# Attention layer on one core: where the matmul operands lie in SBUF, modulo 64 bytes

## The chip, the cores and the metric

The kernel runs on 1 core of one Trainium2 chip (trn2). The metric is device time in microseconds (us). Engines are named as in the profile: PE is TensorE (matmuls), PEld its weight loads, DVE VectorE, ACT ScalarE, POOL GpSimd, SP SyncE. A matmul on PE has a *stationary* operand (128 columns, put into the array by a weight load) and a *moving* operand (up to 512 columns, streamed through it). "fp32r" is a 4-byte type in which PE takes a value in one pass.

## The reference

For each of 32 images x of 1024 tokens by 256 channels, all in float32:

```python
def _L0_conv_ref(inputs, Wq, bq, Wk, bk, Wv, bv, Wo, bo):
    ...
    q = x @ Wq + bq
    k = x @ Wk + bk
    v = x @ Wv + bv
    scores = jnp.einsum('bnc,bmc->bnm', q, k) * scale
    attn = jax.nn.softmax(scores, axis=-1)
    attended = jnp.einsum('bnm,bmc->bnc', attn, v)
    out = attended @ Wo + bo
...
x = x + _L0_conv_ref(_gn(x), ...)
```

`_gn` is a group norm over 32 groups of 8 channels, without learned scale.

## The kernel before

The weights are folded once: a = Wq Wk^T and vo = Wv Wo, so that per image there are four families of matmuls. Each float32 operand is split in two fp32r parts, hi and lo, and each product is the sum of three: hi*hi, hi*lo, lo*hi. h is the normalised image (channels on the partitions), N = 1024 tokens, T = 8 tiles of 128 tokens, K = 2 tiles of 128 channels, CH = 2 chunks c of Q = 512 query tokens, TQ = 4 tiles of 128 queries in a chunk.

| family (function, line) | stationary | moving | matmuls per image | columns moved |
|---|---|---|---|---|
| `project_g` (L626 to L638) | a_hi, a_lo | h_hi, h_lo | 24 | 512 |
| `scores` (L654 to L664) | h_hi, h_lo | g_hi, g_lo | 96 (48 per chunk) | 512 |
| `project_v` (L640 to L652) | h_hi, h_lo | vo_hi, vo_lo | 48 | 256 |
| `attend` (L666 to L683) | p_hi, p_lo | v_hi, v_lo | 192 (24 per query tile) | 258 or 256 |

In `attend` there are three matmuls for each key tile m of 0 to 7: L679 (p_hi with v_hi, 258 columns), L680 (p_hi with v_lo, 256) and L681 (p_lo with v_hi, 258). Column 256 of v_hi is 1.0, so that it sums the softmax's denominator; column 257 is zero. The first three families issue their matmuls in the helper `product` (L593), so their rows have that line; the operands' names tell them apart. A row names the output, then the moving and the stationary operand: `ps_s<-g_hi,h_lo` is a score matmul with h_lo stationary.

The order on PE for image b, written out in `body` (L712 to L728): scores of chunk 0; attend of image b-1, chunk 1; project_v; scores of chunk 1 (with the two small group-statistics products `mean_of_groups` and `variance_of_groups` for image b+1 between); attend of chunk 0; project_g of image b+1. The images run in a loop but for the first and the last.

The other engines work beside it. ACT moves scores out of PSUM into s_buf (L306), computes the exponentials p_hi (L314) and once more in float32 (L320), and the hi parts of h, g and v (L289, L294, L299). DVE computes maxima (L435 and on), subtracts them (L465), takes the lo parts (p_lo L473, h_lo L408, g_lo L415, v_lo L421) and finishes the output (L480, L485). PE waits by semaphore for g_lo ahead of scores (L657, L660), for h_lo ahead of project_g (L629), for v_lo and p_lo ahead of attend (L669, L678).

The buffers are allocated in the order in which `sb(...)` names them (L86 to L125), one after the other from byte 16,512 of each partition, each rounded up to 32 bytes. `minus_half` has 8 bytes and takes 32, and this moves what follows it half of 64 bytes on, until `g_bias`, another one of 8 bytes, moves it back. The places that result, in bytes beyond a multiple of 64:

| buffer | used as | before | changed |
|---|---|---|---|
| a_hi, a_lo | stationary | 32 | 0 |
| h_hi, h_lo | stationary in scores and project_v, moving in project_g | 0 | 0 |
| p_hi, p_lo | stationary | 0 | 0 |
| vo_hi, vo_lo | moving | 32 | 32 |
| g_hi, g_lo | moving | 0 | 32 |
| v_hi, row m | moving | 8m (rows of 1032 bytes) | 32 (rows of 1088 bytes) |
| v_lo, row m | moving | 0 (rows of 1024 bytes) | 32 |
| s_buf, x_t, row_max, top2, out_bias | DVE and ACT only | 0 | 0 |
| o_buf | DVE and DMA | 32 | 32 |

The stationary slices are 512 bytes (128 columns of 4 bytes) at multiples of 512 bytes in their buffer, and the moving slices of g, h, vo and v_lo start at multiples of 1024, so that the table holds for each matmul.

The lines of the allocation that matter:

```python
86         ident = sb("ident", [P, P])
...
89         minus_half = sb("minus_half", [P, K])
90         a_hi = sb("a_hi", [P, K, C], F32R)
...
94         g_bias = sb("g_bias", [P, K])
95         out_bias = sb("out_bias", [P, C])
...
103        v_hi = sb("v_hi", [P, T, VC], F32R)
104        v_lo = sb("v_lo", [P, T, C], F32R)
```

Of the kernel before, what the change touches and what calls it, by code (L numbers as in the profile page):

```python
# [31 lines left out]
F32 = mybir.dt.float32  # L32
F32R = mybir.dt.float32r
# [4 lines left out]
P = 128  # L38
# [4 lines left out]
def attention_kernel(nc, x, x_turned, wq, bq, wk, bk, wv, bv, wo, bo, out):  # L43
    B, H, W, C = x.shape
    N = H * W
    T = N // P
    K = C // P
    CH = 2
    Q = N // CH
# [6 lines left out]
    QB = Q // SQ  # L56
    SB = 4
    VC = C + 2
    SCALE = float(C) ** -0.5


# [3 lines left out]
    with ExitStack() as ctx:  # L65
        def sb(name, shape, dt=F32):
            return ctx.enter_context(nc.sbuf_tensor(name, shape, dt))

        def sem(name):
            return ctx.enter_context(nc.semaphore(name))  # L70
# [15 lines left out]
        ident = sb("ident", [P, P])  # L86
        group_mean = sb("group_mean", [P, P])
        ones = sb("ones", [P, P])
        minus_half = sb("minus_half", [P, K])
        a_hi = sb("a_hi", [P, K, C], F32R)  # L90
        a_lo = sb("a_lo", [P, K, C], F32R)
        vo_hi = sb("vo_hi", [P, K, C], F32R)
        vo_lo = sb("vo_lo", [P, K, C], F32R)
        g_bias = sb("g_bias", [P, K])
        out_bias = sb("out_bias", [P, C])


        x_t = sb("x_t", [P, K, N])
        h_hi = sb("h_hi", [P, K, N], F32R)
        h_lo = sb("h_lo", [P, K, N], F32R)  # L100
        g_hi = sb("g_hi", [P, K, N], F32R)
        g_lo = sb("g_lo", [P, K, N], F32R)
        v_hi = sb("v_hi", [P, T, VC], F32R)
        v_lo = sb("v_lo", [P, T, C], F32R)
        bn_parts = sb("bn_parts", [P, K, 2, 6])
        chan = sb("chan", [P, K, 2])
        g_mean = sb("g_mean", [P, K])
# [5 lines left out]


        s_buf = [sb(f"s_buf{c}", [P, T, Q]) for c in range(CH)]
        p_hi = [sb(f"p_hi{c}", [P, T, Q], F32R) for c in range(CH)]
        p_lo = [sb(f"p_lo{c}", [P, T, Q], F32R) for c in range(CH)]
        top2 = sb("top2", [P, 2, Q])
        top_turned = sb("top_turned", [P, Q])
        part_max = sb("part_max", [P, QB])  # L120
# [17 lines left out]
        const_step = sem("const_step")  # L138
# [44 lines left out]
        def after(eng, semaphore, value):  # L183

            if not isinstance(value, int) or value > 0:
                eng.wait_ge(semaphore, value)

        def nothing(*_):
            pass

        def images(eng, body):

            body(0, True, False)
            with eng.Fori(1, B - 1) as b:
                body(b, False, False)
            body(B - 1, False, True)


        @block.sync
        def _(sp):  # L200
            def load_turned(b):
                after(sp, h_lo_done, b * 2)
                for k in range(K):
                    sp.dma_start(x_t[:, k, :], x_turned[b, k * P:(k + 1) * P, :]).then_inc(xt_landed[k], 16)

            def residual(b, c):

                after(sp, x_copied[c], b * 16)
                sp.dma_start(out_v[b, :, c * TQ:(c + 1) * TQ, :],
                             x_v[b, :, c * TQ:(c + 1) * TQ, :]).then_inc(x_copied[c], 16)  # L210

            def load_weight(n, w, landed):
                sp.dma_start(raw[:, n, :, :], w.rearrange("(k p) n -> p k n", p=P)).then_inc(landed, 16)  # L213

            load_weight(0, wq, wqk_in)
            load_weight(1, wk, wqk_in)
            with nc.allow_non_contiguous_dma(reason="a short vector, once"):
                sp.dma_start(bq_col, bq.rearrange("(k p) -> p k", p=P)).then_inc(wqk_in, 16)
            load_turned(0)
            load_weight(2, wv, wvo_in)  # L220
            load_weight(3, wo, wvo_in)
            with nc.allow_non_contiguous_dma(reason="a short vector, once"):
                sp.dma_start(bv_col, bv.rearrange("(k p) -> p k", p=P)).then_inc(wvo_in, 16)
            sp.dma_start(bo_row, bo.rearrange("(a n) -> a n", a=1)).then_inc(wvo_in, 16)
            residual(0, 0)
            residual(0, 1)

            def body(b, first, last):
                if not last:
                    load_turned(b + 1)  # L230
                    residual(b + 1, 0)
                    residual(b + 1, 1)

            images(sp, body)
            after(sp, x_copied[0], 16 * B)
            after(sp, x_copied[1], 16 * B)
            after(sp, stored[0], 16 * B)
            after(sp, stored[1], 16 * B)


        @block.gpsimd
        def _(pool):
            pool.memset(ident[:], 0.0).then_inc(const_step, 1)
            pool.memset(group_mean[:], 1.0 / GC).then_inc(const_step, 1)
            pool.memset(ones[:], 1.0).then_inc(const_step, 1)
            pool.memset(minus_half[:], -0.5).then_inc(const_step, 1)
            pool.memset(v_hi[:, :, C:C + 1].bitcast(F32), 1.0).then_inc(const_step, 1)
            pool.memset(v_hi[:, :, C + 1:VC].bitcast(F32), 0.0).then_inc(const_step, 1)
            pool.wait_ge(const_step, 6)
            pool.affine_select(out=ident[:], in_=ident[:], compare_op=ALU.not_equal, fill=1.0, base=0,  # L250
                               pattern=[[-1, P]], channel_multiplier=1).then_inc(const_step, 1)
            blocks = group_mean[:].rearrange("p (g c) -> p g c", c=GC)
            pool.affine_select(out=blocks, in_=blocks, compare_op=ALU.is_ge, fill=0.0, base=0,
                               pattern=[[-GC, P // GC], [0, GC]], channel_multiplier=1).then_inc(const_step, 1)
            pool.wait_ge(const_step, 8)
            pool.affine_select(out=blocks, in_=blocks, compare_op=ALU.is_ge, fill=0.0, base=GC - 1,
                               pattern=[[GC, P // GC], [0, GC]], channel_multiplier=-1).then_inc(const_step, 1)

            def store(b, c):

                after(pool, x_copied[c], b * 16 + 16)
                after(pool, o_out, b * 8 + (4 * c + 4))
                pool.dma_start(out_v[b, :, c * TQ:(c + 1) * TQ, :], o_buf[c][:],  # L263
                               accum_op=ALU.add).then_inc(stored[c], 16)

            def inverse_std(b):
                pool.wait_ge(var_done, b + 1)
                pool.tensor_tensor(rstd[:], g_var[:], minus_half[:], ALU.pow).then_inc(rstd_done, 1)

            inverse_std(0)  # L270

            def body(b, first, last):
                if not first:
                    store(b - 1, 1)
                if not last:
                    inverse_std(b + 1)
                store(b, 0)

            images(pool, body)
            store(B - 1, 1)  # L280
# [3 lines left out]
        def _(act):  # L284
# [23 lines left out]
            def exponentials_hi(b, c, i):  # L308

                rows = slice(i * PIECE, (i + 1) * PIECE)  # L310
                if i == 0:
                    after(act, o_ps, b * 8 + (4 * c + 4 - 8))
                act.wait_ge(diff_done, b * 8 + (4 * c + i + 1))
                nc.scalar.activation(p_hi[c][:, rows, :], s_buf[c][:, rows, :], ACT.Exp,  # L314
                                     scale=SCALE).then_inc(p_hi_done, 1)

            def exponentials(b, c, i):

                piece = s_buf[c][:, i * PIECE:(i + 1) * PIECE, :]
                nc.scalar.activation(piece, piece, ACT.Exp, scale=SCALE).then_inc(p_done, 1)  # L320

# [267 lines left out]
        def _(pe):  # L589
# [76 lines left out]
            def attend(b, c, j, last_image=False):  # L666

                if j == 0:
                    pe.wait_ge(v_lo_done, b * 4 + 4)  # L669
                if j >= 2:  # L670

                    after(pe, o_out, b * 8 + (4 * c + j + 1 - 4))
                    if c == 0 and not last_image:
                        pe.wait_ge((spread_done, var_done)[j - 2], b + 2)
                ps, cols = ps_o[j], slice(j * P, (j + 1) * P)
                for m in range(T):
                    if j == 0 and m % PIECE == 0:
                        pe.wait_ge(p_lo_done, b * 8 + (4 * c + m // PIECE + 1))  # L678
                    nc.tensor.matmul(ps[:, 0:VC], p_hi[c][:, m, cols], v_hi[:, m, :], start=m == 0, stop=False)  # L679
                    nc.tensor.matmul(ps[:, 0:C], p_hi[c][:, m, cols], v_lo[:, m, :], start=False, stop=False)  # L680
                    last = nc.tensor.matmul(ps[:, 0:VC], p_lo[c][:, m, cols], v_hi[:, m, :], start=False,  # L681
                                            stop=m == T - 1)
                last.then_inc(o_ps, 1)  # L683

# [46 lines left out]
            for j in range(TQ):  # L731
                attend(B - 1, 1, j)
# [31 lines left out]
```

## Time and profile before

| | |
|---|---|
| median of 3 runs | 1859.79 us (1859.34 to 1862.06) |
| the profiled execution | 1862.75 us, its span 1861.1 us, mean granted clock 0.994 |
| PE busy | 1833.9 us (99% of the span) in 11690 matmuls |
| PEld busy | 1670.2 us (90%) |
| DVE busy | 1642.1 us (88%) |
| ACT busy | 981.8 us (53%) |
| POOL busy | 94.0 us (5%) |
| DMA | 101.92 MB, mean 55 GB/s |

Matmuls are pipelined: a row's duration is longer than the time until the next one starts (0.39 us against 0.23 us for 512 columns). What a matmul takes of the span is therefore read from start to start, in the timeline, and not from its mean duration. The granted clock is given in shares of 2.4 GHz.

### The profile page before, as it was taken

To read this page: it belongs to the slowest core of one execution; us is meant where nothing else is said; L and a number is where in the kernel's file an instruction comes from. 1 tells how busy PE (TensorE), PEld (TensorE's weight loads), DVE (VectorE), ACT (ScalarE), POOL (GpSimd) and SP (SyncE) were. 2 spreads that over 40 slices of the span, in tenths; PEclk is the share of its full clock that TensorE was granted. 3 is DMA by queue.
4 is the path that set the end of the run, shared out by engine and by line. 5 is a ranking of instruction groups with operands and counts; after the bars stand their busy time and mean duration, and the time that the engine had idled before them with its cause. 6 is when DMAs were issued, how large, how long until landed. Compare 5 with 4: busy or idle time off the path is not lost.

```text
span 1861.1 us, 33031 instructions
## 1 busy us (share of the span) xinstructions
PE 1833.9 (99%) x11690; PEld 1670.2 (90%) x11690; DVE 1642.1 (88%) x2793; ACT 981.8 (53%) x1347; POOL 94.0 (5%) x109
## 2 busy tenths in 40 slices
PE   8899999999999999999999999999999999999997
PEld 7799998998998998989999989989889999899896
DVE  5898998988988989989889889889899898898885
ACT  3545545546546455456455465465564554654652
POOL 0000000000000000000000000000000000000000
PEclk9899999999999999999999999999999999999998
DMA  3211212202222112222122222132221122220211
GB/s 113 57 44 36 68 56 68 68 19 60 68 56 68 55 24 68 56 68 68 32 47 68 56 68 62 17 68 60 64 68 36 42 68 56 68 67 12 67 23 24
DMA packets 29296, 101.92 MB, mean 55 GB/s; under 512 B 3681, under 2 KB 4706, under 8 KB 29282
## 3 DMA queue, kind: packets, MB, share of 16 engines
q0 software_dynamic: 9216, 33.56, 11.6%
q1 hardware_dynamic: 20066, 68.17, 11.2%
q8 instruction: 9, 0.15, 0.0%
q14 instruction: 5, 0.04, 0.0%
HBM read 68.16 MB, written 67.11 MB: 73 GB/s over the span
## 4 chain that ended last, share of the span: by engine, by line
PE 98%; DVE 1%; ACT 0%; DMA 0%; issue 0%; SPq 0%; POOLq 0%
PE ps_s L593 48%; PE ps_o L681 13%; PE ps_o L679 13%; PE ps_o L680 13%; PE ps_o L593 10%; DMA s_buf<-in_L_conv_bq_dram 0%; ACT p_hi L314 0%; ACT s_buf L320 0%; DVE s_buf L465 0%; DVE p_lo L473 0%; PE ps_o L605 0%; DVE s_buf L490 0%; DVE query_max L452 0%; PE ps_s L605 0%; SPq L213 0%
## 5 line engine op out<-in xcount | busy, mean ns | idle before, releaser
L679 PE MATMUL ps_o<-v_hi,p_hi 128*128 128x258 f32 x2048 | 580.5, 283 | 3.2 <-DVE p_lo L473 3.2
L681 PE MATMUL ps_o<-v_hi,p_lo 128*128 128x258 f32 x2048 | 582.0, 284 | 0.0
L680 PE MATMUL ps_o<-v_lo,p_hi 128*128 128x256 f32 x2048 | 578.1, 282 | 0.0
L314 ACT ACTIVATE p_hi<-s_buf 128x1024 fp32r<-128x1024 f32 x256 | 272.1, 1063 | 527.2 <-DVE s_buf L465 527.2
L593 PE MATMUL ps_s<-g_hi,h_hi 128*128 128x512 f32 x1024 | 406.3, 397 | 7.5 <-ACT s_buf L306 7.5
L593 PE MATMUL ps_s<-g_hi,h_lo 128*128 128x512 f32 x1024 | 400.8, 391 | 0.0
L593 PE MATMUL ps_s<-g_lo,h_hi 128*128 128x512 f32 x1024 | 399.6, 390 | 0.0
L679 PEld LDWEIGHTS ps_o<-v_hi,p_hi 128*128 128x128 f32 x2048 | 387.5, 189 | 6.1 <-issue 2.2
L680 PEld LDWEIGHTS ps_o<-v_lo,p_hi 128*128 128x128 f32 x2048 | 389.7, 190 | 2.8
L306 ACT ACTIVATE s_buf<-ps_s 128x512 f32<-128x512 f32 x512 | 293.6, 608 | 185.5 <-PE ps_s L593 182.8
L681 PEld LDWEIGHTS ps_o<-v_hi,p_lo 128*128 128x128 f32 x2048 | 388.5, 190 | 0.0
L473 DVE TENSOR_TENSOR p_lo<-s_buf,p_hi 128x1024 fp32r<-128x1024 f32 x256 | 304.3, 1219 | 22.7 <-ACT s_buf L320 22.7
L465 DVE TENSOR_TENSOR s_buf<-s_buf,row_max 128x1024 f32<-128x1024 f32 x256 | 306.5, 1218 | 1.1
L320 ACT ACTIVATE s_buf<-s_buf 128x1024 f32<-128x1024 f32 x256 | 271.1, 1059 | 0.0
L593 PEld LDWEIGHTS ps_s<-g_hi,h_hi 128*128 128x128 f32 x1024 | 192.9, 188 | 45.9 <-ACT s_buf L306 7.8
L435 DVE TENSOR_TENSOR top<-top,s_buf 128x512 f32<-128x512 f32 (+1 forms) x192 | 166.8, 869 | 75.4 <-ACT s_buf L306 64.1
L593 PEld LDWEIGHTS ps_s<-g_hi,h_lo 128*128 128x128 f32 x1024 | 192.7, 188 | 42.0
L593 PEld LDWEIGHTS ps_s<-g_lo,h_hi 128*128 128x128 f32 x1024 | 193.1, 189 | 37.1
L485 DVE SCALAR_TENSOR_TENSOR o_buf<-ps_o,rden,out_bias 128x256 f32<-128x256 f32 x256 | 123.9, 484 | 14.4
L263 POOL DMA_DIRECT2D out_dram<-o_buf x64 | 55.9, 874 | 1366.7 <-DVE o_buf L485 1349.5
L299 ACT ACTIVATE v_hi<-ps_o 128x512 fp32r<-128x512 f32 x64 | 38.4, 600 | 107.3 <-PE ps_o L593 107.3
L435 DVE TENSOR_TENSOR top<-s_buf 128x1024 f32<-128x1024 f32 x64 | 78.4, 1225 | 12.1 <-ACT s_buf L306 12.1
(86 smaller groups left out, 2213.4 us busy)
## 6 DMA issues: line engine op xcount, KB each, us to landing
x_t<-in_x_turned_dram SPq DMA_DIRECT2D x64, 512.0 KB, 4.0
out_dram<-in_x_dram SPq DMA_DIRECT2D x64, 512.0 KB, 7.6
out_dram<-o_buf POOLq DMA_DIRECT2D x64, 512.0 KB, 5.4
s_buf<-in_L_conv_Wq_dram SPq DMA_DIRECT2D x1, 256.0 KB, 3.1
s_buf<-in_L_conv_Wk_dram SPq DMA_DIRECT2D x1, 256.0 KB, 3.1
s_buf<-in_L_conv_Wv_dram SPq DMA_DIRECT2D x1, 256.0 KB
s_buf<-in_L_conv_Wo_dram SPq DMA_DIRECT2D x1, 256.0 KB
s_buf<-in_L_conv_bq_dram SPq DMA_DIRECT2D x1, 1.0 KB, 4.0
```

Of the source, the lines that this page charges most:

```text
L263: pool.dma_start(out_v[b, :, c * TQ:(c + 1) * TQ, :], o_buf[c][:], accum_op=ALU.add).then_inc(stored[c], 16)
L306: nc.scalar.activation(s_buf[c][:, m, :], ps_s[(8 * c + m) % SB][:], ACT.Copy).then_inc(s_out, 1)
L314: nc.scalar.activation(p_hi[c][:, rows, :], s_buf[c][:, rows, :], ACT.Exp, scale=SCALE).then_inc(p_hi_done, 1)
L320: nc.scalar.activation(piece, piece, ACT.Exp, scale=SCALE).then_inc(p_done, 1)
L435: nc.vector.tensor_tensor(to, left, right, ALU.max).then_inc(top_step, 1)
L465: nc.vector.tensor_tensor(piece, piece, row_max[:].unsqueeze(1).broadcast_to([P, PIECE, Q]), ALU.subtract).then_inc(diff_done, 1)
L473: nc.vector.tensor_tensor(p_lo[c][:, rows, :], s_buf[c][:, rows, :], p_hi[c][:, rows, :].bitcast(F32), ALU.subtract).then_inc(p_lo_done, 1)
L485: nc.vector.scalar_tensor_tensor(out=o_buf[c][:, j, :], in0=ps_o[j][:, 0:C], scalar=rden[:, t:t + 1], in1=out_bias[:], op0=ALU.mult, op1=A ...
L593: last = nc.tensor.matmul(ps, stationary, moving, start=start and n == 0, stop=stop and n == len(pairs) - 1)
L679: nc.tensor.matmul(ps[:, 0:VC], p_hi[c][:, m, cols], v_hi[:, m, :], start=m == 0, stop=False)
L680: nc.tensor.matmul(ps[:, 0:C], p_hi[c][:, m, cols], v_lo[:, m, :], start=False, stop=False)
L681: last = nc.tensor.matmul(ps[:, 0:VC], p_lo[c][:, m, cols], v_hi[:, m, :], start=False, stop=m == T - 1)
```

## The change

The allocation is reordered. First come the buffers that are stationary in some matmul (and x_t), from a multiple of 64 bytes; then a filler `shift` of 32 bytes; then the buffers that are only moving operands (vo, g, v_hi, v_lo); then a filler `shift_back` of 32 bytes, and the rest. A row of v_hi is 272 columns (1088 bytes, 17 times 64) in place of 258 (1032 bytes); the matmuls still read the first 258, and the start-up memset of the columns behind the ones is 15 columns wide in place of 1. No instruction is added, dropped or moved on any engine, and all shapes on PE, DVE and ACT stay.

```diff
+    VROW = 272
...
-        minus_half = sb("minus_half", [P, K])
+
         a_hi = sb("a_hi", [P, K, C], F32R)
         a_lo = sb("a_lo", [P, K, C], F32R)
-        vo_hi = sb("vo_hi", [P, K, C], F32R)
-        vo_lo = sb("vo_lo", [P, K, C], F32R)
-        g_bias = sb("g_bias", [P, K])
-        out_bias = sb("out_bias", [P, C])
-
-
         x_t = sb("x_t", [P, K, N])
         h_hi = sb("h_hi", [P, K, N], F32R)
         h_lo = sb("h_lo", [P, K, N], F32R)
+        p_hi = [sb(f"p_hi{c}", [P, T, Q], F32R) for c in range(CH)]
+        p_lo = [sb(f"p_lo{c}", [P, T, Q], F32R) for c in range(CH)]
+
+        sb("shift", [P, 8])
+        vo_hi = sb("vo_hi", [P, K, C], F32R)
+        vo_lo = sb("vo_lo", [P, K, C], F32R)
         g_hi = sb("g_hi", [P, K, N], F32R)
         g_lo = sb("g_lo", [P, K, N], F32R)
-        v_hi = sb("v_hi", [P, T, VC], F32R)
+        v_hi = sb("v_hi", [P, T, VROW], F32R)
         v_lo = sb("v_lo", [P, T, C], F32R)
+        sb("shift_back", [P, 8])
+
+        minus_half = sb("minus_half", [P, K])
+        g_bias = sb("g_bias", [P, K])
+        out_bias = sb("out_bias", [P, C])
...
-        p_hi = [sb(f"p_hi{c}", [P, T, Q], F32R) for c in range(CH)]
-        p_lo = [sb(f"p_lo{c}", [P, T, Q], F32R) for c in range(CH)]
...
-            pool.memset(v_hi[:, :, C + 1:VC].bitcast(F32), 0.0).then_inc(const_step, 1)
+            pool.memset(v_hi[:, :, C + 1:VROW].bitcast(F32), 0.0).then_inc(const_step, 1)
...
-                    nc.tensor.matmul(ps[:, 0:VC], p_hi[c][:, m, cols], v_hi[:, m, :], start=m == 0, stop=False)
+                    nc.tensor.matmul(ps[:, 0:VC], p_hi[c][:, m, cols], v_hi[:, m, 0:VC], start=m == 0, stop=False)
...
-                    last = nc.tensor.matmul(ps[:, 0:VC], p_lo[c][:, m, cols], v_hi[:, m, :], start=False,
+                    last = nc.tensor.matmul(ps[:, 0:VC], p_lo[c][:, m, cols], v_hi[:, m, 0:VC], start=False,
```

## Rows read from the trace of the kernel before

**Rows 1.** The page: engines' busy time, and the chain of waits by engine and line

```profile
PE 1833.9 (99%) x11690; PEld 1670.2 (90%) x11690; DVE 1642.1 (88%) x2793; ACT 981.8 (53%) x1347; POOL 94.0 (5%) x109
...
PE 98%; DVE 1%; ACT 0%; DMA 0%; issue 0%; SPq 0%; POOLq 0%
```

**Rows 2.** Timeline of PE: first matmul of six stages; start us, duration us, name, count

```profile
887.21 0.29 PE L679 MATMUL ps_o<-v_hi,p_hi 128*128 128x258 f32 x1
...
898.74 0.28 PE L593 MATMUL ps_o<-vo_hi,h_hi 128*128 128x256 f32 x1
...
904.42 0.40 PE L593 MATMUL ps_s<-g_hi,h_hi 128*128 128x512 f32 x1
...
915.85 0.29 PE L679 MATMUL ps_o<-v_hi,p_hi 128*128 128x258 f32 x1
...
927.37 0.40 PE L593 MATMUL ps_o<-h_hi,a_hi 128*128 128x512 f32 x1
...
932.98 0.39 PE L593 MATMUL ps_s<-g_hi,h_hi 128*128 128x512 f32 x1
...
943.88 0.29 PE L679 MATMUL ps_o<-v_hi,p_hi 128*128 128x258 f32 x1
```

**Rows 3.** Timeline of PE: one query tile of attend, L679 of key tiles 0, 1, 3, 4, 5

```profile
892.96 0.28 PE L679 MATMUL ps_o<-v_hi,p_hi 128*128 128x258 f32 x1
...
893.33 0.28 PE L679 MATMUL ps_o<-v_hi,p_hi 128*128 128x258 f32 x1
...
894.05 0.28 PE L679 MATMUL ps_o<-v_hi,p_hi 128*128 128x258 f32 x1
...
894.42 0.28 PE L679 MATMUL ps_o<-v_hi,p_hi 128*128 128x258 f32 x1
...
894.77 0.29 PE L679 MATMUL ps_o<-v_hi,p_hi 128*128 128x258 f32 x1
```

**Rows 4.** Busy time by stretch: attend, then project_g; us, busy (count) by engine, clock

```profile
915.90:927.30 11.40, 11.40 (x97) 11.40 (x96) 10.44 (x22) 2.61 (x3) 0.31 (x1) 1.00 0.00 0
927.40:932.90 5.50, 5.50 (x26) 4.41 (x25) 5.43 (x10) 5.00 (x7) 0.28 (x1) 1.00 0.86 257
```

**Rows 5.** Timeline of PE at the start-up: float32 products in several passes, 256 columns

```profile
16.76 3.19 PE L593 MATMUL ps_s<-s_buf 128*128 128x256 f32 x7
...
19.75 0.63 PE L593 MATMUL ps_o<-s_buf,o_buf 128*128 128x256 f32 x1
```

**Rows 6.** Timeline of DVE beside project_g: start us, duration us, name, count

```profile
924.42 2.31 DVE L408 TENSOR_TENSOR h_lo<-x_t,h_hi 128x1024 fp32r<-128x1024 f32 x2
...
931.91 0.74 DVE L415 SCALAR_TENSOR_TENSOR g_lo<-ps_o,g_bias,g_hi 128x512 fp32r<-128x512 f32 x1
```

**Rows 7.** The waits of PE: waited for, us in total, times, longest us

```profile
PE ps_s L593 <- ACT s_buf L306: 7.5, 1, 7.5
...
PE ps_o L605 <- DMA s_buf<-in_L_conv_bq_dram: 6.0, 1, 6.0
...
PE ps_o L679 <- DVE p_lo L473: 3.2, 2, 2.0
```

**Rows 8.** Timeline of POOL at the start, and the first work of PE

```profile
1.43 0.11 POOL L248 MEMSET v_hi<- 128x8 f32 x1
...
5.98 1.97 PE L605 MATMUL ps_o<-ident,s_buf 128*128 128x128 f32 x8 [5.98 <-DMA s_buf<-in_L_conv_bq_dram]
```

## The prediction

> **What bounds the kernel now.** The page says it at once: PE is busy for 99% of the span, and the chain of work that ended last is PE for 98% of it [rows 1]. PE's list of waits is short; its three longest entries make 16.7 us in all, two of them single events at the start [rows 7]. So what a change does to the time here, it does through how quickly one matmul follows another on PE.
>
> That pace is read from the start times [rows 2], one image in its six stages, each from its first matmul to the next stage's first. Attend of chunk 1: 887.21 to 898.74, 11.53 us for 96 matmuls, 120.1 ns each. project_v: 5.68 us for 48, 118.3 ns. Scores of chunk 1: 11.43 us for 48 and the two small statistics products between them. Attend of chunk 0: 11.52 us for 96, 120.0 ns. project_g: 5.61 us for 24, 233.8 ns. Scores of chunk 0: 932.98 to 943.88, 10.90 us for 48, 227.1 ns. An image takes 56.67 us.
>
> The granted clock is 1.00 of 2.4 GHz [rows 4]. At a column per cycle 512 columns would take 213.3 ns, 256 columns 106.7, and attend's average of 257.3 (two of 258, one of 256) 107.2. What is left over is an **excess per matmul**. Beside it I set the places of the operands modulo 64 bytes, from the table above:
>
> - scores, 512 columns, stationary at 0, moving at 0: 227.1 - 213.3 = 13.8 ns
> - project_g, 512 columns, stationary at 32, moving at 0: 233.8 - 213.3 = 20.5 ns
> - project_v, 256 columns, stationary at 0, moving at 32: 118.3 - 106.7 = 11.6 ns
> - attend, 257.3 columns, stationary at 0, moving at 0 (v_lo) or 8m (v_hi): 120.05 - 107.2 = 12.85 ns
>
> Within attend, the key tiles differ. In one query tile [rows 3] tile m = 0, all operands at 0, takes 893.33 - 892.96 = 0.37 us for its three matmuls. Tile 3, with v_hi at 24, also takes 0.37, and tile 4, with v_hi at 32, only 0.35. The 24 matmuls of this tile (the next query tile starts at 895.85) have nothing else that differs between m = 0 and m = 4. The rows' last digit is 0.01 us, so 0.35 is 115 to 118 ns per matmul, which with rounding on both ends I take as 117.7, an excess of 10.5 ns; 0.37 is 123, an excess near 15. That is the same as for scores (13.8) with twice the columns at the same places.
>
> So the excess reads like a toll per pair of weight load and matmul, not per column, and it depends on where the two operands lie: about 14 to 15 for (0, 0), about 11 for (0, 32), about 20 for (32, 0). The start-up has a stretch without it: seven float32 products of 256 columns, four passes each, take 19.75 - 16.76 = 2.99 us, 427 ns each, which is 4 times 106.7 [rows 5]. There PE draws its moving values at a quarter of the rate beside the loads. The toll seems to be paid where both operands are read from SBUF at full rate.
>
> **The Trainium skill against this.** Its page "TensorE: Matmul & The Clock Gate", section "Part 2: What happens when you issue a matmul", says that TensorE has two independent read ports into SBUF, and that loading the next weights takes no bandwidth from the running matmul. By that rule no place modulo 64 could matter and the change would do nothing; this trace speaks against it, as project_g and scores, of equal shape, differ by 6.7 ns. The page "SBUF — State Buffer", section "Specifications (TRN2)", has 16-byte lines; by it only v_hi's odd rows (8m no multiple of 16) would cross more lines, tile 4 would not differ from tile 0, and little would be won. Tiles 0 and 4 do differ [rows 3].
>
> **The change, part by part.** No instruction is added or moved, so the sum is four families by their new excess. For (stationary 0, moving 32) I have two prices, 11.6 from project_v and 10.5 from key tile 4, and take 11.1.
>
> 1. *attend*, 192 times 32 = 6144 matmuls, goes to (0, 32) throughout: 107.2 + 11.1 = 118.3 in place of 120.05, which is 1.75 ns each, **-10.8 us**. Bounds: 118.8 (project_v's excess), -7.7 us; 116.7 (0.35 us by three), -20.6 us.
> 2. *scores*, 3072 matmuls, g moves from 0 to 32: 213.3 + 11.1 = 224.4 in place of 227.1, 2.7 ns each, **-8.3 us**. This is the term that no row shows: 512 columns at (0, 32). Bounds: below, twice the gain, -16.6 us, if the wider matmul profits for both halves of its stream; above, 233.8, project_g's price, which is also a pair 32 bytes apart, +20.6 us. I take the value near project_v and tile 4, because (0, 0) costs about the same at 512 and at 256 columns, so the width doesn't seem to matter.
> 3. *project_g*, 24 times 32 = 768 matmuls, goes from (32, 0) to (0, 0), because a moves down and h is the moving operand there: 227.1 in place of 233.8, 6.7 ns each, **-5.1 us**. Bounds: 0 if it is the stream h that is dear there, -6 if the toll were 12.9 as in attend.
> 4. *project_v* is (0, 32) before and after: 0.
> 5. *The memset* at the start is wider (15 columns of 8 rows for 1) in an operation of 0.11 us at 1.43; PE starts at 5.98 with the weights' DMA [rows 8]. Even tenfold it ends before. Cost 0, and were the cover gone, at most the 1 us that it grows.
> 6. *DVE and ACT* keep their shapes; g_lo, g_hi, v_lo and v_hi are written 32 bytes on. No row tells the two places of one buffer apart there. I set it at 0: it hides in the slack that follows, and what goes beyond that slack is paid in full.
>
> **What is late next.** DVE is busy 10.44 of 11.40 us beside attend and 5.43 of 5.50 beside project_g [rows 4], and its chain there starts from the last score tile, not from attend. The second g_lo ends at 931.91 + 0.74 = 932.65, and the first score matmul, which waits for it (L657), starts at 932.98: 0.33 us of slack. h_lo ends at 924.42 + 2.31 = 926.73 and project_g starts at 927.37: 0.64 us [rows 6, 2]. The change takes 96 times 1.75 ns = 0.17 us from attend and 24 times 6.7 = 0.16 us from project_g, 0.33 together: the whole slack of g_lo, and no more. If attend came to 116.7 (0.32 us), scores would wait 0.15 us per image, about 5 us in all of the further gain given back.
>
> **Sum.** -10.8 - 8.3 - 5.1 = -24.2 us on the profiled execution, 1862.75 to 1838.6. The median before was 1859.79, 3.0 lower, so the forecast is **1836 us**.
>
> **The rivals.**
>
> *R1, slower: what counts at 512 columns is that the operands are 32 apart.* The only 512-column rows with places 32 apart are project_g's, and they are the slow ones. If the order of the two doesn't matter, then scores, the largest family by columns, turns from 227.1 to 233.8, +20.6 us; project_g gains its 5.1, and attend at project_v's price 7.7: +7.8, that is 1868 us. It decides from the point where a score matmul passes 227.1 + (10.8 + 5.1)/3072 = 232.3 ns. For it: project_g; and 118.3 of project_v doubled is 236.6. Against: the toll of (0, 0) doesn't grow with the columns. Chance 0.20.
>
> *R2, scores stay.* Their pace of 227.1 is the steadiest in the trace and may be a floor of its own for 512 columns. Then only attend and project_g gain: -15.9, 1844 us. Chance 0.13.
>
> *R3, no change.* The tolls follow from something else than the place modulo 64 (higher address bits, the order of the streams), and all buffers move there too, so that gains and losses cancel, or the change doesn't make the difference it states: 1860 us. Against: tile 4 against tile 0, of the same buffers. Chance 0.12.
>
> *R4, the toll goes away.* (0, 32) keeps the two readers apart once all matmuls have it, and the excess falls to 2 or 3 ns as in the start-up's passes [rows 5]: 11 ns from each score matmul and 10 from each of attend would be 1.06 us per image in scores and 0.96 in each attend; of the attend ahead of project_g only the 0.33 us of g_lo's slack can be had, so (1.06 + 0.96 + 0.33) times 32 = 75 us, 1785 us. Against: project_v, 48 in a row at (0, 32), has 11.6. Chance 0.03.
>
> **How the numbers follow.** The forecast itself has 0.52. A measurement of this kernel can tell from no change what is over about 0.2%, 3.7 us. The forecast, R2 and R4 are faster by more: 0.68. R3 is the same: 0.12. R1 is slower: 0.20. The range goes down to 1817, the forecast with attend at 116.7, scores at twice the gain and project_g's 5.1 (-42.3), and up to R1's 1868, of which half lies above; with R4 and the rest of R1 out, some 0.15 is left out. Since cases of both signs are in it: the forecast's own range is 1817 to 1848.
>
> **What would show each step.** In the timeline of PE of the changed kernel, from start to start: attend about 11.36 us for 96 matmuls in place of 11.53, and all key tiles alike (0.35 or 0.36); scores of chunk 0 about 10.77 in place of 10.90; project_g about 5.45 in place of 5.61; project_v still 5.68. An image then takes about 55.9 us in place of 56.67. Scores above 10.95 us say R1; scores at 10.90 with the rest as forecast say R2; all stages as before say R3. A wait of PE for DVE's g_lo, not in the list now, says that the slack was spent. The forecast is wrong if project_v moves, as its places modulo 64 stay, or if key tiles still differ.

## The result and the profile after

The changed kernel takes 1868.47 us (median of 6 runs, 1865.65 to 1869.53) against 1860.94 us of the kernel before (6 runs, 1859.34 to 1862.46): a ratio of 1.004, with a 95% interval of 1.0028 to 1.0052. It is 7.5 us slower. The profiled execution took 1869.22 us, with a span of 1867.6 us and a mean granted clock of 0.995.

The page has PE where it was, at 99% of a longer span, with 7.5 us more of busy time; DVE and ACT are where they were [rows 1]:

```profile
PE 1841.4 (99%) x11690; PEld 1661.5 (89%) x11690; DVE 1644.2 (88%) x2793; ACT 982.5 (53%) x1347; POOL 94.1 (5%) x109
```

The timeline of PE, one image, the first matmul of each stage as in [rows 2] (columns: start us, duration us, name, count):

```profile
946.85 0.28 PE L683 MATMUL ps_o<-v_hi,p_hi 128*128 128x258 f32 x1
...
958.29 0.28 PE L597 MATMUL ps_o<-vo_hi,h_hi 128*128 128x256 f32 x1
...
963.95 0.39 PE L597 MATMUL ps_s<-g_hi,h_hi 128*128 128x512 f32 x1
...
975.57 0.28 PE L683 MATMUL ps_o<-v_hi,p_hi 128*128 128x258 f32 x1
...
987.03 0.40 PE L597 MATMUL ps_o<-h_hi,a_hi 128*128 128x512 f32 x1
...
992.54 0.46 PE L597 MATMUL ps_s<-g_hi,h_hi 128*128 128x512 f32 x1
...
1003.80 0.28 PE L683 MATMUL ps_o<-v_hi,p_hi 128*128 128x258 f32 x1
```

The differences of these starts, beside those of the kernel before and of two kernels that come below (g_back and v64, read in the same way, one image each):

| stage (us) | before | changed | g_back | v64 |
|---|---|---|---|---|
| attend, chunk 1 | 11.53 | 11.44 | 11.47 | 11.32 |
| project_v | 5.68 | 5.66 | 5.60 | 5.44 |
| scores, chunk 1 | 11.43 | 11.62 | 11.43 | 11.39 |
| attend, chunk 0 | 11.52 | 11.46 | 11.47 | 11.31 |
| project_g | 5.61 | 5.51 | 5.51 | 5.66 |
| scores, chunk 0 | 10.90 | 11.26 | 11.01 | 11.02 |
| image | 56.67 | 56.95 | 56.49 | 56.14 |

In this image the score stages lose 0.19 and 0.36 us; everything else gains, 0.27 us together. Added up from start to start over all images, scores went from 707.9 to 724.5 us (+16.6), attend from 744.0 to 739.2 (-4.8), project_g from 179.5 to 176.3 (-3.2), project_v from 181.8 to 180.4 (-1.4): +7.2 us. The two profiled executions differ by 6.5 us and the medians by 7.5.

The time between g_lo and the scores has shrunk, too. DVE's rows beside project_g [rows 6]: the second g_lo ends at 991.63 + 0.74 = 992.37, the first score matmul starts at 992.54, 0.17 us later where it was 0.33.

```profile
984.14 2.32 DVE L412 TENSOR_TENSOR h_lo<-x_t,h_hi 128x1024 fp32r<-128x1024 f32 x2
...
991.63 0.74 DVE L419 SCALAR_TENSOR_TENSOR g_lo<-ps_o,g_bias,g_hi 128x512 fp32r<-128x512 f32 x1
```

That already costs a little. The first score matmul lasts 0.46 us in place of 0.39, and the second follows it only after 0.30 us:

```profile
992.54 0.46 PE L597 MATMUL ps_s<-g_hi,h_hi 128*128 128x512 f32 x1
992.84 0.39 PE L597 MATMUL ps_s<-g_lo,h_hi 128*128 128x512 f32 x1
```

Over the images this first gap averages 276 ns, against 232 ns in only_g (below), whose scores run at the same pace and whose g_lo is early. So about 1.4 of the 16.6 us that scores lose are a wait, and the rest is their pace. In every kernel here the second score matmul starts 0.46 us or more after the end of g_lo. Before the change it started 0.55 to 0.60 us after it, so that only some 0.10 us of the 0.33 could be had.

### The profile page after: what moved, and what is told of

It is laid out like the page before. It is cut to its first block, busy times and chain, and to the rows that moved or that the text cites. A ratio compares the mean times of both kernels' runs of the same rounds, so it can differ in the third digit from the quotient of the medians.

```text
span 1867.6 us, 33031 instructions
## 1 busy us (share of the span) xinstructions
PE 1841.4 (99%) x11690; PEld 1661.5 (89%) x11690; DVE 1644.2 (88%) x2793; ACT 982.5 (53%) x1347; POOL 94.1 (5%) x109
## 4 chain that ended last, share of the span: by engine, by line
PE 98%; DVE 1%; ACT 0%; DMA 0%; issue 0%; SPq 0%; POOLq 0%
PE ps_s L597 49%; PE ps_o L683 13%; PE ps_o L685 13%; PE ps_o L684 13%; PE ps_o L597 10%; DMA s_buf<-in_L_conv_bq_dram 0%; ACT p_hi L318 0%; ACT s_buf L324 0%; DVE s_buf L469 0%; DVE p_lo L477 0%; PE ps_o L609 0%; DVE s_buf L494 0%; DVE query_max L456 0%; PE ps_s L609 0%; SPq L217 0%
## 5 line engine op out<-in xcount | busy, mean ns | idle before, releaser
L597 PE MATMUL ps_s<-g_hi,h_hi 128*128 128x512 f32 x1024 | 411.3, 402 | 7.4 <-ACT s_buf L310 7.4
L597 PE MATMUL ps_s<-g_hi,h_lo 128*128 128x512 f32 x1024 | 405.2, 396 | 0.0
L597 PE MATMUL ps_s<-g_lo,h_hi 128*128 128x512 f32 x1024 | 405.1, 396 | 0.0
```

The lines of the kernel that those rows point to most:

```text
L597: last = nc.tensor.matmul(ps, stationary, moving, start=start and n == 0, stop=stop and n == len(pairs) - 1)
```

## The experiments

"Distance" below is the moving operand's start minus the stationary operand's, in bytes. Three theories stood at first. D: the distance modulo 64 sets the pace. P: any operand off a multiple of 64 costs. T: the toll of the forecast, one price per pair whatever the width. The ratios are of each kernel's runs to those of the kernel before on the same chip. Each kernel of blocks ran once.

### Blocks of equal matmuls: distance or place

The attention is replaced by 35 blocks of 48 matmuls, each with one width and one pair of places:

```diff
+            for i, (cols, s, d, wide) in enumerate(CONFIGS):
+                for n in range(COUNT):
+                    last = nc.tensor.matmul(banks[i % 8][0:wide, 0:cols], left[:, s:s + wide], right[:, d:d + cols],
+                                            start=n == 0, stop=n == COUNT - 1)
+                last.then_inc(done, 1)
```

> Leaves the whole attention out: it copies x to the output and runs 35 blocks of 48 matmuls on constant data, each block with its own width and places of the two operands modulo 64 bytes. Theory D (distance): the pace of a 512-column matmul depends on the distance of the two operands modulo 64. Then (0,0) and (32,32) take 227 ns, (0,32) and (32,0) take 233 to 234. Theory P (place): an operand that starts off a multiple of 64 costs more. Then (32,32) takes 234 or more, up to 240. Theory T (toll per pair, as forecast): (0,32) takes 224 ns. For 256 columns D and P expect 117 to 120 for all, with little between them; T expects 118 for (0,32) and 121 for (0,0).

Timeline of PE within six blocks, 512 columns each (start, time from the first start to the last end, count). The pace is that time less one duration of 0.39 us, by the count less one:

```profile
21.22 5.29 PE L83 MATMUL ps<-right,left 128*128 128x512 f32 x22
...
32.18 5.76 PE L83 MATMUL ps<-right,left 128*128 128x512 f32 x24
...
43.71 5.15 PE L83 MATMUL ps<-right,left 128*128 128x512 f32 x22
...
120.72 6.11 PE L83 MATMUL ps<-right,left 128*128 128x512 f32 x26
...
132.24 5.73 PE L83 MATMUL ps<-right,left 128*128 128x512 f32 x24
...
290.83 5.60 PE L83 MATMUL ps<-right,left 128*128 128x512 f32 x24
```

In order: (stationary 0, moving 32) 4.90/21 = 233 ns; (32, 0) 5.37/23 = 233 ns; (32, 32) 4.76/21 = 227 ns; (0, 64) 5.72/25 = 229 ns; (0, 128) 5.34/23 = 232 ns; (0, 0) 5.21/23 = 227 ns. (32, 32) is as quick as (0, 0), and the two mixed pairs are equal: at 512 columns **it is the distance, and P falls**. T falls with (0, 32), for which it had 224. And a multiple of 64 is not enough: a distance of 128 costs 5 ns, while 256 and 512 bytes gave 226.6, as 0 did.

From the start times of the last 24 matmuls of each block:

| columns | distance 0 | 32 | -32 | 64 | 128 | 256 |
|---|---|---|---|---|---|---|
| 512 | 226.7 ns | 233.3 | 233.2 | 228.7 | 232.2 | 226.6 |
| 384 | 173.3 | 173.3 | | | | |
| 256 | 120.0 | 117.7 | 118.2 | 113.4 | 118.6 | 120.0 |

At 256 columns the order turns round: a distance of 32 is better than 0 by 2.3 ns, and 64 is better by 6.6. Three lines of the same view show it, 256 columns at distance 0, 64 and 128, with durations of 0.28 us: 2.16/18 = 120, 2.26/20 = 113 and 2.26/19 = 119 ns.

```profile
174.33 2.44 PE L83 MATMUL ps<-right,left 128*128 128x256 f32 x19
...
231.39 2.54 PE L83 MATMUL ps<-right,left 128*128 128x256 f32 x21
...
236.83 2.54 PE L83 MATMUL ps<-right,left 128*128 128x256 f32 x20
```

### g alone moved

The kernel before, with a filler on each side of g:

```diff
+        sb("shift", [P, 8])
         g_hi = sb("g_hi", [P, K, N], F32R)
         g_lo = sb("g_lo", [P, K, N], F32R)
+        sb("shift_back", [P, 8])
```

> The kernel before with g alone moved 32 bytes on. Theory D and theory P: scores go from 227 to 233.3 ns, 5.2 to 6 ns on 3072 matmuls, 16 to 18 us slower, and attend, project_v and project_g stay. If the loss of the change sits elsewhere (in attend's new rows or in DVE), this kernel is no more than 5 us slower.

1874.83 us, ratio 1.0076 (1.0061 to 1.0092): 13.6 us slower. Scores of chunk 0 in its timeline of PE: 1006.46 - 995.27 = 11.19 us in place of 10.90.

```profile
995.27 0.39 PE L595 MATMUL ps_s<-g_hi,h_hi 128*128 128x512 f32 x1
...
1006.46 0.28 PE L681 MATMUL ps_o<-v_hi,p_hi 128*128 128x258 f32 x1
```

Scores add up to 723.3 us, 15.5 more; attend got 1.9 us of waits back. So g's 32 bytes by themselves cost more than the whole change loses; its other parts gain.

### g back at a multiple of 64

```diff
+        g_hi = sb("g_hi", [P, K, N], F32R)
+        g_lo = sb("g_lo", [P, K, N], F32R)
         sb("shift", [P, 8])
         vo_hi = sb("vo_hi", [P, K, C], F32R)
         vo_lo = sb("vo_lo", [P, K, C], F32R)
-        g_hi = sb("g_hi", [P, K, N], F32R)
-        g_lo = sb("g_lo", [P, K, N], F32R)
```

> The changed kernel with g back at a multiple of 64 bytes, all else as changed. Theory D and P: scores return to 227 ns, 16 us less than the changed kernel, 1852 to 1853 us, 8 us faster than before: attend's 0.7 ns on 6144 matmuls and project_g's 4.2 ns on 768 stay as gains. If scores were slowed by something else than g's place, it stays near 1868 us.

1854.83 us, ratio 0.9966 (0.9954 to 0.9978): faster than before by 6.4 us and than the changed kernel by 13.6. That is 2 us short of what was expected. The last column but one of the stage table shows where: scores of chunk 0 take 11.01 us, not 10.90. After project_g at its new pace the second g_lo comes just too late: in all images but one the first score matmul starts 0.13 or 0.14 us after it, and the next one follows after 0.33 us in place of 0.23. That is 0.10 us in nearly every image, 3 us. The weight loads (PEld) show what is late: the load of the first score matmul, which before started 0.21 us ahead of its matmul (932.77 for 932.98, [rows 2]), now starts with it, at 984.48 for 984.49.

The kernel before:

```profile
932.77 0.19 PEld L593 LDWEIGHTS ps_s<-g_hi,h_hi 128*128 128x128 f32 x1
```

g_back:

```profile
984.48 0.19 PEld L597 LDWEIGHTS ps_s<-g_hi,h_hi 128*128 128x128 f32 x1 [0.25 <-issue]
...
984.49 0.49 PE L597 MATMUL ps_s<-g_hi,h_hi 128*128 128x512 f32 x1
984.82 0.39 PE L597 MATMUL ps_s<-g_lo,h_hi 128*128 128x512 f32 x1
```

### All operands at distance 0 modulo 64

The changed kernel without the filler `shift` ahead of vo (it stands behind v_lo):

```diff
-        sb("shift", [P, 8])
         vo_hi = sb("vo_hi", [P, K, C], F32R)
...
         v_lo = sb("v_lo", [P, T, C], F32R)
+        sb("shift", [P, 8])
         sb("shift_back", [P, 8])
```

> The changed kernel with every matmul operand at a multiple of 64 bytes, rows of v_hi 1088 bytes apart. Theory D: scores and project_g 227 ns as in g_back; attend and project_v at distance 0. If 256 columns behave as 512 do, attend and project_v gain too, down to 113.5 ns, 4 to 6 ns on 7680 matmuls, 1815 to 1825 us. If key tile 4 of the kernel before (v_hi at 32) showed the better place, attend goes to 121 ns, 10 us above g_back. If 256 columns do not care, it equals g_back, 1852 us.

1858.51 us, ratio 0.9984 (0.9975 to 0.9993), 3.7 us slower than g_back. project_v goes to 120.0 ns, as the block of 256 columns at distance 0 does (g_back: 116.7); attend stays, 119.3 ns without its waits, against 119.5. The hope that 256 columns behave as 512 do fell, and so did the 121 ns for attend.

### v alone moved

The kernel before with v_hi and v_lo at distance 32 modulo 256, as the changed kernel has them:

```diff
+    VROW = 272
...
-        v_hi = sb("v_hi", [P, T, VC], F32R)
+        sb("shift", [P, 40])
+        v_hi = sb("v_hi", [P, T, VROW], F32R)
         v_lo = sb("v_lo", [P, T, C], F32R)
+        sb("shift_back", [P, 40])
```

> The kernel before with v_hi and v_lo alone moved to 32 bytes past a multiple of 64 (and 32 past the stationary operand modulo 256, as in the changed kernel), rows of v_hi 1088 bytes apart; g, a and vo stay. Theory D: scores and project_g stay at 227 and 233.5 ns; attend takes the changed kernel's 119.4 in place of 120.1 ns, 4.3 us faster in all, 1856 to 1857 us. The forecast's toll had attend at 118.3, 10.8 us faster, 1850 us.

1858.99 us, ratio 0.9989 (0.9979 to 0.9998). That is 1.6 us less than the kernel before on the same chip, with an interval from 0.4 to 3.9; attend adds up to 740.8 us, 3.2 less. So v's part of the change is worth 2 to 3 us, not the forecast's 10.8.

### A distance that is a multiple of 64, but not of 256

g_back with g 128 bytes on:

```diff
+        sb("away", [P, 32])
         g_hi = sb("g_hi", [P, K, N], F32R)
         g_lo = sb("g_lo", [P, K, N], F32R)
+        sb("away_back", [P, 32])
```

> The kernel g_back with g moved 128 bytes on: still a multiple of 64, but 128 from h modulo 256. If only the distance modulo 64 counted, nothing changes, 1854.8 us. By the blocks (232.2 ns at a distance of 128 bytes) scores lose 4 to 5 ns on 3072 matmuls, 12 to 15 us: 1867 to 1870 us.

1866.94 us, ratio 1.0033 (1.002 to 1.0046), 12 us slower than g_back, where the distance modulo 64 had it unchanged. Scores of chunk 0 take 1000.88 - 989.68 = 11.20 us. The rule "modulo 64" of the change's own words is too coarse.

```profile
989.68 0.44 PE L599 MATMUL ps_s<-g_hi,h_hi 128*128 128x512 f32 x1
...
1000.88 0.28 PE L685 MATMUL ps_o<-v_hi,p_hi 128*128 128x258 f32 x1
```

### More blocks, and project_v at 192

> Leaves the whole attention out, as the first block kernel, with 36 other blocks; all places are multiples of 64 bytes but for a few near 64. The first block kernel had 256 columns at 120.0 ns for a distance of 0, 256 and 512 bytes, 118.6 for 128 and 113.4 for 64. Theory D256: what counts is the distance modulo 256 bytes. Then 64, 320 and 576 bytes take 113.4 ns, 192, 448 and 704 take another common value, and a stationary operand at 64 with a moving one at 128 (distance 64) takes 113.4 too. Theory place: only a moving operand at 64 bytes itself is fast, and (64, 128) takes 120. For 258 columns, as attend has them, D256 expects about 114.2 at 64 bytes if the two extra columns cost their 0.8 ns only, and 119 to 120 if the pattern is broken by them. 512 columns at distance 64 repeat 228.7.

Timeline of PE in two of these blocks of 256 columns, distances 192 and 320 (2.49/22 = 113 and 2.47/21 = 118 ns):

```profile
13.33 2.77 PE L84 MATMUL ps<-right,left 128*128 128x256 f32 x23
...
18.99 2.75 PE L84 MATMUL ps<-right,left 128*128 128x256 f32 x22
```

At 512 columns the distance modulo 256 sets the pace in all of these blocks. (64, 64) took 226.7 ns as (0, 0) did; (32, 96) took 229.0, the same as (0, 64) in this kernel; (128, 0) took 232.1, as (0, 128) had; (0, 192) and (64, 0), which is 192 modulo 256, took 233.4 both.

At 256 columns it is not so simple. Moving places of 192, 448 and 704 with the stationary operand at 0 all took 113.35 ns, but (64, 0), the same distance modulo 256, took 117.8. 320 and 576 took 117.8, though 64 had taken 113.4 in the first kernel of blocks. (0, 64) itself stood at the start of this kernel: its first 25 matmuls followed one another at about 213 ns, and the rest at 117.8. So the very same places gave 113.4 and 117.8 ns, and how a stretch is entered matters. (64, 128), which was to decide, took 117.8 too, where one theory had 113.4 and the other 120: both fell. No run tells whether (64, 0) differs from (0, 192) by its places or by the block ahead of it. 258 columns at 64 bytes took 118.6, where 114.2 was hoped for: the two extra columns spoil it.

The kernel g_back with vo at 192:

```diff
-        sb("shift", [P, 8])
+        sb("shift", [P, 48])
         vo_hi = sb("vo_hi", [P, K, C], F32R)
         vo_lo = sb("vo_lo", [P, K, C], F32R)
+        sb("more", [P, 24])
```

> The kernel g_back with vo at a distance of 192 bytes from h modulo 256, where blocks of 256 columns took 113.35 ns. project_v then goes from 116.7 to 113.4 ns if it falls into that pattern, 3.3 ns on 1536 matmuls, 5 us faster, 1850 us. If the pattern depends on how the stretch is entered, 117.8 ns, 1.6 us slower than g_back.

1849.22 us, ratio 0.9933 (0.9919 to 0.9946), 5.6 us faster than g_back. project_v takes 954.11 - 948.66 = 5.45 us for 48, and after its first three matmuls each follows at 113 or 114 ns.

```profile
948.66 0.28 PE L598 MATMUL ps_o<-vo_hi,h_hi 128*128 128x256 f32 x1
...
954.11 0.39 PE L598 MATMUL ps_s<-g_hi,h_hi 128*128 128x512 f32 x1
```

### v at 16 bytes: a miss

g_back with v_hi, v_lo and vo starting 4 columns into buffers of their own, and rows of v_hi 1280 bytes apart:

```diff
-    VROW = 272
+    VROW = 320
...
+        def past(name, rows, width, by=4):
+            whole = sb(name, [P, rows * width + 64], F32R)
+            return whole[:, by:by + rows * width].rearrange("p (r w) -> p r w", w=width)
```

> The kernel g_back with v_hi, v_lo and vo 16 bytes past the place of the stationary operand modulo 256 (rows of v_hi 1280 bytes apart), where blocks of 256 and 258 columns took 116.6 and 116.8 ns. Attend then goes from 119.4 to 116.8 ns. Of the 0.25 us per image that the attend ahead of project_g gains, only the 0.13 us that g_lo is early are had, of the other attend all: 12 us faster than g_back, 1843 us. If the three different operands of attend break the pattern, attend stays at 119 to 120 ns and the time within 3 us of g_back.

1875.85 us, ratio 1.008 (1.0066 to 1.0094). Blocks of 256 and 258 columns had taken 116.6 and 116.8 ns at this distance. attend fell into a pattern of 126, 128 and 119 ns and stayed in it, 124 ns on average: here the blocks' pace did not carry over.

The kernel shows one thing more. As attend is slow, g_lo comes 0.51 us ahead of the first score matmul, and chunk 0's scores take 10.88 us, the least of all kernels with g at distance 0. That fits the 11.01 us in g_back as a wait.

### Attend's triple in blocks, then in the kernel

```diff
+                    cols, d = (256, d2) if n % 3 == 1 else (258, d1 + step * (n // 3 % 8))
```

> Leaves the whole attention out, as the block kernels. Each block of 60 matmuls repeats attend's triple: 258, 256 and 258 columns with the stationary operand at 0, the 258-column ones d1 and the 256-column one d2 past it, d1 and d2 of 0, 32, 64, 128 and 192 bytes; five more blocks have 16 bytes, or v_hi's place moving on by 64 bytes from one triple to the next as rows of 1088 bytes do. Attend in the changed kernel takes 119.4 ns. If one row of places is as good for the triple as 192 bytes is for 256 columns alone (113.4 ns), it shows a mean of 115 or less here; if the two extra columns spoil every pattern, as in the blocks of 258 columns, all means lie from 117 to 124 ns. If the order of places matters and not the distance alone, the block of 16 bytes is slow here, at 124, as attend was in v16.

The 30 means lie from 115.6 to 122.2 ns. All four blocks in which v_hi's place moves on by 64 bytes per triple, as rows of 1088 bytes do, have 119.4 to 119.7 over their last 24 gaps, whatever the first distance: that is attend's pace in the changed kernel. With v_hi standing still modulo 256, (32, 32) gives 117.9 and (64, 192) gives 117.8. The block of 16 bytes was the best here, at 115.6, and did not show the 124 of v16. Both good pairs went into the kernel vo192:

```diff
-    VROW = 272
+    VROW = 320
```

and, for the second, more fillers around v_hi and v_lo:

```diff
-        sb("more", [P, 24])
+        sb("more", [P, 32])
         v_hi = sb("v_hi", [P, T, VROW], F32R)
+        sb("more_yet", [P, 32])
         v_lo = sb("v_lo", [P, T, C], F32R)
-        sb("shift_back", [P, 8])
+        sb("shift_back", [P, 32])
```

> The kernel vo192 with rows of v_hi 1280 bytes apart, so that all operands of attend lie 32 bytes past the stationary one modulo 256 for every key tile. In the blocks of triples that took 117.9 ns, against 119.4 to 119.6 for rows that move on by 64 bytes each (and 119.46 in vo192's attend). If the blocks carry over: 1.5 ns on 6144 matmuls, 9 us faster than vo192's 1849 us, 1840 us, with at most 1 us of it given back in a wait for g_lo. If attend keeps a pattern of its own, as in v16, it may be anywhere from 117 to 124 ns, 1835 to 1877 us.

> As row1280, with v_hi 64 and v_lo 192 bytes past the stationary operand modulo 256; in the blocks of triples 117.8 ns, the same as row1280's 117.9. If the blocks carry over, both kernels end within 2 us of each other near 1840 us. If they part by more, blocks of a single stationary slice do not tell what attend does.

row1280: 1850.75 us, ratio 0.9941 (0.9927 to 0.9954). v64: 1842.99 us, ratio 0.9901 (0.9886 to 0.9917), **18.9 us faster than the kernel before**. attend does what the blocks said in both, 117.9 and 117.8 ns. In row1280's timeline its key tiles are all alike at last, 0.35 or 0.36 us each; in the changed kernel they still differ, 0.35 to 0.37:

```profile
945.31 0.28 PE L684 MATMUL ps_o<-v_hi,p_hi 128*128 128x258 f32 x1
...
945.66 0.28 PE L684 MATMUL ps_o<-v_hi,p_hi 128*128 128x258 f32 x1
...
946.02 0.28 PE L684 MATMUL ps_o<-v_hi,p_hi 128*128 128x258 f32 x1
...
946.37 0.28 PE L684 MATMUL ps_o<-v_hi,p_hi 128*128 128x258 f32 x1
```

The changed kernel, the same line:

```profile
949.69 0.28 PE L683 MATMUL ps_o<-v_hi,p_hi 128*128 128x258 f32 x1
...
950.05 0.29 PE L683 MATMUL ps_o<-v_hi,p_hi 128*128 128x258 f32 x1
...
950.42 0.28 PE L683 MATMUL ps_o<-v_hi,p_hi 128*128 128x258 f32 x1
```

row1280 missed its 1840 us: it is 1.5 us slower than vo192. Its attend gained 10.1 us (739.6 to 729.5), but project_v lost 6.3 (174.6 to 180.9) and project_g with the wait behind it 4.8 (176.2 to 181.0).

Why do row1280 and v64 part by 7.8 us? project_v has the same places in both, but comes in from another pattern of attend: in row1280 it runs at 117.8 ns, in v64 at 113.6, 180.9 against 174.5 us. These are the two paces that the blocks showed too. v is also written to other places in the two kernels; no run takes that apart from the way in.

In both the gain of the attend ahead of project_g is given back in a wait for g_lo. In v64's timeline of PE, project_g's last matmul starts at 978.45 and the first of scores at 978.87: 0.42 us for 0.227. Its g_lo ends at 978.00 + 0.74 = 978.74. The second score matmul then follows only after 0.33 us, as in g_back.

```profile
978.45 0.39 PE L599 MATMUL ps_s<-h_hi,a_lo 128*128 128x512 f32 x1
978.87 0.49 PE L599 MATMUL ps_s<-g_hi,h_hi 128*128 128x512 f32 x1
979.20 0.40 PE L599 MATMUL ps_s<-g_lo,h_hi 128*128 128x512 f32 x1
```

```profile
978.00 0.74 DVE L421 SCALAR_TENSOR_TENSOR g_lo<-ps_o,g_bias,g_hi 128x512 fp32r<-128x512 f32 x1
```

That is 0.19 us ahead of the scores and 0.10 us behind the first of them, 0.29 us in nearly every image, 9 us. From here on, DVE's order beside project_g sets part of the time.

## Why the prediction was wrong

**The step that failed is term 2, scores**: forecast -8.3 us, measured +16.6. It took the toll of (0, 32) from 256-column rows and carried it to 512 columns, on the ground that "(0, 0) costs about the same at 512 and at 256 columns, so the width doesn't seem to matter". That ground holds in the blocks, and says nothing of other distances: (0, 0) has 13.3 ns at 256, 384 and 512 columns, but a distance of 32 has 11.1, 13.3 and 20.0. The only 512-column rows with unequal places were project_g's, 20.5 ns [rows 2], and the forecast read them as a matter of which operand was off. The blocks show both orders at 233 ns.

**Rival R1 was what happened**, with its mechanism, and its time of 1868 us within 0.5 us. Its deciding point was 232.3 ns per score matmul; without the jumps at the statistics products they took 233.2. It had been given 0.20, and the range ended at its number, so that the result lies just outside. That its total is so near is partly luck: scores lost 16.6 us where R1 had 20.6, and attend and project_g gained 8.0 together where R1 had 12.8.

*Term 1, attend*: -10.8 forecast, -4.8 measured, 119.4 ns for 118.3. The price came from key tile 4 against tile 0 [rows 3]. But with v_hi at 32 modulo 64 throughout, the tiles still differ: their three matmuls take 354 to 365 ns on average over the images, where it was 353 to 366. The forecast looked at places modulo 64 alone. Modulo 256, tile 0 of the kernel before was no (0, 0): v_hi lay 128 + 8m and v_lo 192 bytes past p. And 1088-byte rows keep moving v_hi on by 64 modulo 256. That a tile's time also carries what the tiles before it left behind is likely from the blocks, but not shown for a single tile. "All key tiles alike" was wrong for the changed kernel and right for row1280.

*Term 3, project_g*: -5.1 forecast, -3.2 measured. It does reach 227 ns, but only after its first 11 matmuls (224 to 240 ns on the way), and there are only 24 in a row.

*Term 4, project_v*: 0 forecast, -1.4 measured, 118.3 to 117.4 ns with its places modulo 64 unchanged. Modulo 256 they did change: vo lay 32 bytes before h's place and now lies 32 bytes past it. The blocks have 118.2 ns for the one and 117.7 for the other, and only_v, which keeps the old places but has the new rows of v, stays at 118.5. The way in has a part as well: g_back, with the changed kernel's places, runs at 116.7.

*Terms 5 and 6*, the memset and the writes of DVE and ACT, were rightly at nothing: DVE's busy time is 1644.2 us for 1642.1.

*What is late next* named the right wait and had its size wrong. Of the 0.33 us between g_lo and the scores only some 0.10 could be had, since the second score matmul never starts sooner than 0.46 us after g_lo. The changed kernel pays 1.4 us for it in the time of its scores, g_back 3, and v64 9, where the forecast had nothing up to 0.33 us. PE's list of waits doesn't show it; the start times do.

*The Trainium skill.* The page "TensorE: Matmul & The Clock Gate", section "Part 2: What happens when you issue a matmul", has two independent SBUF read ports for the two operands. By that alone their distance should not matter. For fp32r it does: between one distance and another, blocks of equal 512-column matmuls differ by 6.6 ns each. The 16-byte lines of "SBUF — State Buffer", section "Specifications (TRN2)", don't explain it either, since all the places in the table above are multiples of 16. Off them, blocks of 256 columns took 126.7 ns at 8 bytes, but 120.0 to 120.1 at 24, 40 and 56, as at 0.

**What stays open.** No run shows what in the chip repeats with 256 bytes, or why the pace depends on history. That the weight load and the moving stream disturb each other is the reading of the start-up's undisturbed passes [rows 5] and of the dependence on distance at 512 columns; no run took the weight loads away.

## What to carry to other kernels

Where back-to-back fp32r matmuls with a weight load each bound the kernel, the distance of the two operands in SBUF is a tuning knob worth about 1%, and it has to be set for each width by itself: here a multiple of 256 bytes for 512 columns and 192 for 256, where 64 was as good in one block and not in others. A price read at one width or one pair of places is no price for another; make blocks of the very shape first, and then run them in the kernel, because a stretch also takes on the pattern of the one before it. And when PE is sped up, look how early each operand is ready, counted to the weight load and not to the matmul: here 0.33 us of slack were in truth 0.10, and a gain turned into a wait.

## What the runs showed of the hardware that was not expected

The paces are spaced in steps. At the granted clock of 1.00 (2.4 GHz), 16 columns take 6.67 ns, which are 64 bytes of the moving operand. Several of the steady blocks lie a whole number of these above a column per cycle: 512 columns at 226.7 (two) and 233.3 (three), 384 at 173.3 (two), 256 at 113.35 (one) and 120.0 (two). Others, such as 117.8 for 256 columns, lie between.

A stretch of 512 columns at distance 0 needs up to 11 matmuls to settle, when it comes in from another pace: 3 to 10 in the blocks, 11 in the changed kernel's project_g. Scores before the change show the same after each of the two statistics products: 229, 233, 236, 224, 231, 236, 228, 233, 231 ns and then 227, some 40 ns more for the nine than at 227 each. A two-column product in the middle of a stage thus costs more than its own time.
